# Shifting score rows inside SBUF: each four-tile group by itself, four rows per transfer, in place of two rows over eight tiles

## The reference

```
AC = einsum('bhid,bhjd->bhij', q + u_bias, k)
BD = einsum('bhid,hjd->bhij', q + v_bias, rp)
BD = _rel_shift(BD)                       # row i of BD is shifted by an amount that depends on i
attn = softmax((AC + BD) * scale, axis=-1)
out = einsum('bhij,bhjd->bhid', attn, v)
```

## Time and profile before

| What | Value |
|---|---|
| median of three executions | 3201.2 us (3196.62 to 3203.26) |
| the profiled execution, its own time | 3208.71 us |
| its span, first to last instruction | 3206.9 us |
| mean granted TensorE clock | 0.948 |
| TensorE busy | 91% of the span |
| VectorE busy | 82% |
| ScalarE busy | 78% |
| GpSimd busy (nearly all of it DMA issues of L663) | 72% |
| the shifts' share of the 16 DMA engines | 62.1% of the span |

### The profile page before, as it was taken

How to read it: one execution, slowest core, us unless ns; L and a number is a source line. 1 busy time by engine, 2 the same in 40 slices (tenths; PEclk the granted TensorE clock), 3 DMA queues, 4 the chain that set the end, 5 groups by cost and what they waited for, 6 DMA issues and landing times. The chain is left out here.

```text
span 3206.9 us, 110520 instructions
## 1 busy us (share of the span) xinstructions
PE 2906.8 (91%) x40768; PEld 2051.1 (64%) x40768; DVE 2634.9 (82%) x5042; ACT 2496.0 (78%) x3850; POOL 2310.1 (72%) x4135
## 2 busy tenths in 40 slices
PE   4655479999999999998999999999999999999955
PEld 1444237777777676776777776777767777777645
DVE  2555149899999899997999998999989999999976
ACT  2333368898888898987888898988888889889732
POOL 3333388888888878887878888888878888888800
PEclk8777679999999999999999999999999999999977
DMA  6233678888888878887888888888888888888831
GB/s 201 86 111 111 137 204 224 224 229 229 227 231 222 231 214 228 222 230 194 227 220 227 227 227 220 228 226 224 225 222 223 227 227 226 228 225 222 214 123 53
DMA packets 290222, 657.31 MB, mean 205 GB/s; under 512 B 189473, under 2 KB 256929, under 8 KB 272289
## 3 DMA queue, kind: packets, MB, share of 16 engines
q0 software_dynamic: 190960, 526.89, 62.1%
q1 hardware_dynamic: 98736, 123.38, 13.2%
HBM read 77.19 MB, written 46.14 MB: 38 GB/s over the span
## 5 line engine op out<-in xcount | busy, mean ns | idle before, releaser
L663 POOL DMA_DIRECT2D score<-score x3999 | 2178.4, 548 | 512.4 <-ACT score L902 442.3
L900 ACT COPY score<-pos_bank 128x512 f32<-128x512 f32 x2048 | 1104.2, 597 | 305.1 <-PE pos_bank L776 303.1
L910 ACT ACTIVATE score<-score,low 128x1024 f32<-128x1024 f32 x1024 | 1197.0, 1170 | 36.3 <-DVE low L963 30.2
L972 DVE COPY prob_t<-pt_bank 128x512 f32<-128x512 f32 x1792 | 1162.2, 684 | 7.9 <-PE pt_bank L842 4.0
L842 PE MATMUL pt_bank<-ident_sb,score 128*128 128x128 f32 x8192 | 1085.4, 275 | 10.8 <-issue 6.5
L842 PEld LDWEIGHTS pt_bank<-ident_sb,score 128*128 128x128 f32 x8192 | 953.5, 142 | 218.2 <-DVE prob_t L972 47.2
L963 DVE CUSTOM_DVE_ANT_0 score<-ac_bank,score 128x1024 f32<-128x1024 f32 x512 | 627.1, 1225 | 245.4 <-PE ac_bank L828 126.7
L776 PE MATMUL pos_bank<-pos,qv 96*32 96x512 bf16 (+15 forms) x12160 | 661.2, 317 | 49.9 <-DMA qv<-qv_parts 42.8
L963 DVE CUSTOM_DVE_ANT_0 score<-ac_bank,score,low 128x1024 f32<-128x1024 f32 x512 | 657.2, 1284 | 56.4 <-PE ac_bank L828 47.6
L856 PE MATMUL acc_bank<-prob_t,vs 128*32 128x128 f32 x16384 | 663.5, 279 | 3.5 <-issue 3.4
L828 PE MATMUL ac_bank<-ks,qu 96*128 96x512 bf16 x2048 | 623.9, 386 | 24.7 <-DVE low L963 24.4
(11 more groups left out here) (95 smaller groups left out, 995.6 us busy)
## 6 DMA issues: line engine op xcount, KB each, us to landing
score<-score POOLq DMA_DIRECT2D x3937, 129.5 KB, 5.1
pos<-pos_parts SPq DMA_DIRECT2D x96, 128.0 KB, 8.5
qv<-qv_parts SPq DMA_DIRECT2D x192, 64.0 KB, 7.2
ks<-k_parts SPq DMA_DIRECT2D x192, 64.0 KB, 7.3
qu<-qu_parts SPq DMA_DIRECT2D x192, 64.0 KB, 7.1
v_heads<-v_sb SPq DMA_DIRECT2D x8, 1024.0 KB, 7.3
vs<-v_heads SPq DMA_DIRECT2D x32, 256.0 KB, 8.0
pos_parts<-part SPq DMA_DIRECT2D x16, 384.0 KB, 3.0
```

Of the source, the lines that this page charges most:

```text
L663: pool.dma_start(shifted(odd, s, groups, 0), shifted(odd, s, groups, QUAD - 1 - s))\
L900: act.copy(score[:, at + f, c * BANK:(c + 1) * BANK], ring(m)[:, :]).then_inc(pos_out, 1)
L910: act.activation(cols, cols, ACT.Exp, bias=low[:, slot(k), NH - 1:NH], scale=-1.0)\
L972: dve.tensor_copy(prob_t[:, c, :], PT[c % 2][:, :]).then_inc(copied, 1)
```

## The change

`move` now shifts group j alone, all four partitions with the same s (s, 32 + s, 64 + s, 96 + s) in one transfer: 4 partitions x 1 group, again 4 pieces of 33,152 bytes. Four semaphores, one for each group of the ring, take the place of the four of the even and odd strips. The added last call goes away, so GpSimd issues 128 x 31 = 3968 transfers and not 3999. `add` waits once, for the transfers of its own group. Nothing else is changed.

```
-            moved = [[sem(f"moved{i}_{'even' if odd == 0 else 'odd'}") for i in range(RING // 2)] for odd in range(2)]
+            moved = [sem(f"moved{i}") for i in range(RING)]
...
             def rows_moved(step, n):
-                return (step * (NT // FT // RING) + n // 2 + 1) * (16 * MOVES)
+                return (step * (NT // FT // RING) + n // RING + 1) * (16 * MOVES)
...
             @block.gpsimd
             def _(pool):
-                def shifted(odd, s, groups, first):
-
-                    rows = score[odd * QUAD + s::2 * QUAD, :, :].rearrange("p (g f) w -> p g (f w)", f=FT)
-                    return rows[:, groups, first:first + (FT - 1) * MWIN + L]
-
-                def move(step, j, last=False):
-
-                    if not last:
-                        wait_apart(pool, pos_out, group(step, j) * ITEMS + ITEMS)
-                    odd = 1 if last else 1 - j % 2
-                    n = (j + 1) // 2 if odd else j // 2
+                def move(step, j):
+
+                    wait_apart(pool, pos_out, group(step, j) * ITEMS + ITEMS)
                     at = j % RING
-                    if last or j == 0 and isinstance(step, int) and step == 0:
-                        groups = slice(at, at + 1)
-                    elif at == 0:
-                        groups = slice(0, RING, RING - 1)
-                    else:
-                        groups = slice(at - 1, at + 1)
                     for s in MOVE_ORDER:
                         if s < QUAD - 1:
-                            pool.dma_start(shifted(odd, s, groups, 0), shifted(odd, s, groups, QUAD - 1 - s))\
-                                .then_inc(moved[odd][n % 2], 16)
-                for j in range(RING):
-                    move(0, j)
+                            rows = score[s::QUAD, at * FT:(at + 1) * FT, :].rearrange("p f w -> p (f w)")
+                            width = (FT - 1) * MWIN + L
+                            pool.dma_start(rows[:, 0:width], rows[:, QUAD - 1 - s:QUAD - 1 - s + width])\
+                                .then_inc(moved[at], 16)
                 with pool.Fori(0, STEPS) as step:
-                    for j in range(RING, RING + NT // FT):
+                    for j in range(NT // FT):
                         move(step, j)
-                for j in range(RING, GROUPS - STEPS * (NT // FT)):
+                for j in range(GROUPS - STEPS * (NT // FT)):
                     move(STEPS, j)
-                move(STEPS, GROUPS - STEPS * (NT // FT) - 1, last=True)
...
                     if h == 0 and k % FT == 0:
-                        for odd in range(2):
-                            n = (k // FT + odd) // 2
-                            dve.wait_ge(moved[odd][n % 2], rows_moved(step, n))
+                        dve.wait_ge(moved[k // FT % RING], rows_moved(step, k // FT))
```

## The result

The changed kernel takes 3439.1 us (median of four executions, 3404.5 to 3448.6) where the kernel before takes 3202.2 beside it: a ratio of 1.071, 95% interval 1.068 to 1.075. It is 237 us slower; the forecast was 64. The sign was right and the time lies in the stated range, but the size and the reason for it were wrong.

The account below looks back on a forecast made before the run. TensorE with its partners bounds the kernel before; after the change the DMA engines would, at 15.5 x 1.25 + 1.9 = 21.3 us per group. That swallows the savings and adds 64 to 3201: 3265 us, range 3155 to 3520.

Parts of the forecast that it names:

- Bound of the kernel before: TensorE with its partners at 20.37 us: In the attention, TensorE with its partners sets the pace, 20.37 us per undisturbed group of four tiles; DMA engines nearest behind.
- Start, -15.6: VectorE's first addition needs only call 0 of the shifts, so it moves from 433.04 to about 417.4: -15.6 us.
- Waits in the steady part, -20: VectorE's 47.3 us of waits for shifts all go, as calls come one period earlier; worth -20 us, bounds 0 and -47.
- Instructions, 0: GpSimd issues 31 fewer transfers and VectorE's second wait goes, worth nothing; an issue stays at 547 ns.
- Rival C: GpSimd needs longer to issue for four engines than for two, up to 682 ns: 3317 us; chance 0.04.
- The transfers' engine time, factor 1.25: Shifts' DMA engine time per MB rises by a factor of 1.25, from 60 to about 75 us; ends 1.0 and 2.0.
- quarter of the crowding of the operand loads: Operand loads crowded on 16 neighbouring partitions took a factor of 2.0; a quarter of that extra was taken for the shifts.
- "More than 20.7, the DMA engines are the bound", +64: DMA work of 21.3 us per group exceeds 20.7, so the last group's addition waits for its shifts: +64 us, savings swallowed.
- rival A: The DMA engines don't hinder each other, factor under 1.20, both savings stand: 3166 us; chance 0.36.
- What would show it: Signs: about 75 us per MB, DMA share 0.97, landings over 5.1, VectorE's waits over 100 us, GpSimd's shorter, TensorE less busy.
- B: The shifts' engine time rises by the full factor of 2.0, 32.9 us per group: 4750 us; chance 0.08.

Follow-up runs that it names:

- before_start: Kernel before, but call 0 shifts all four strips of group 0 and call 1 the rest of group 1, then as before; ratio 1.001.
- after_three: Changed kernel with the fourth tile of each group left unshifted, so it leaves work out; ratio 0.992.
- after_small_loads: Changed kernel with operand loads of q, k and positions cut to 64 columns after the first two in each loop pass; ratio 0.999.
- near: Kernel before with rows s and 32 + s (or 64 + s and 96 + s) in one transfer, in place of rows 64 apart; ratio 1.236.
- before_cross: Kernel before with transfers pairing rows s with 96 + s, and 32 + s with 64 + s; ratio 1.001.
- before_pairs: Kernel before with only the order of the transfers changed, to s = 0, 1, 4, 5, ... 28, 29, then 2, 3, 6, 7, ...; ratio 1.184.
- after_tile: Changed kernel with each piece of 33,152 bytes cut into pieces of 8,192 bytes; ratio 1.068.
- before_sems: Kernel before with ten increments of a semaphore nobody waits for behind each turn on TensorE, 160 to a group; slower by 38%.

## Why the prediction was right or wrong

- *Bound of the kernel before: TensorE with its partners at 20.37 us.* Right, and it stays so: the undisturbed groups of the changed kernel take 20.37 as well.
- *Start, -15.6.* Half right: -10.6. The issue was as forecast, but the landings of the first call took 10.5 us (median of the issues between 393 and 412) and not 5.1. The prediction said that one more microsecond could be borne. It was worth nothing in the end: ten groups later the changed kernel is 17.3 us behind (657.62 against 640.28), and before_start shows the gain given back even where the calls behind land as before.
- *Waits in the steady part, -20.* The waits went, all of them, as forecast. They were worth at most 0.8% together with the start and a clock of 1.00 (after_three), and nothing in after_small_loads.
- *Instructions, 0.* Right; 560 ns and not 547, 17.4 us of 20.4. The fewer issues and the fewer waits cost and brought nothing that shows. Rival C is out.
- *The transfers' engine time, factor 1.25.* Right: 1.20, 72.7 us/MB, just over the 72 below which the forecast would have been wrong. The cause, two engines at one place of a side of 64, is shown by near, before_cross and before_pairs. The prediction's quarter of the crowding of the operand loads was a guess that came near, at 1.25; the figure of the Trainium skill's page, 1.22, was nearer.
- *"More than 20.7, the DMA engines are the bound", +64: this is the step that failed.* The work of the engines was forecast at 21.3 us a group, and it is (0.817 + 0.112) x 22.87 = 21.2. Two misses cancel in that: the shifts' factor was 1.20, and the other queues, carried over at 1.9 us, took 0.112 x 22.87 = 2.6, since the hardware queue's engine time rose too, from 56.6 to 74.7 us per MB (0.101 x 2300 x 16 / 49.73). With 1.20 and 1.9 the sum would have given 20.5 us and no loss, rival A; with 21.2 it gives 394 + 128 x 21.2 + 6 = 3114 and +52. So even with the measured work the step misses most of the 237, and that 3439 lies in the range is luck. For the engines did not become the bound: their share is 0.93, VectorE never waits for a shift, GpSimd's wait for the copies grew from 381 to 523 us where it was to shrink, and a group takes 22.87 us, 1.6 more than the engines need. The cost reached the time by another way, which the prediction did not have among its rivals: longer landings, TensorE standing still for its code for 1.30 us more a group, and its clock at half for 8.5% of the time, which makes 0.83 us more busy time. A queue that is nearly full was treated as harmless until it is full. After_three at 0.91 without loss and after_tile at 0.98 with no more loss than the changed kernel show that the share of the engines, on which the sum was built, is not the measure.
- *What would show it.* Right: engine time per MB, landings over 5.1, TensorE's busy share. Wrong: DMA share of 0.97, VectorE's wait over 100 us, GpSimd's shorter wait. Those three wrong signs say that the mechanism is another, though the sign of the time was right.

Rival A, no hindrance, fails on the 1.20; its own threshold was a factor under 1.20, so the measured one lies right on it, and its 3166 us would still have been wrong. B would have needed 2.0.

## What to carry to other kernels

Put the transfers that run at the same time on different places: rows on both sides of partition 64, and neighbours in the queue four rows apart as in the kernel before; with the same bytes and the same number of transfers, the pairing of rows was worth 24% here and their order 18%. Where the DMA engines are as busy as here (0.84 in the kernel before), read the longest landing and the engines' idle time that ends in "issue" before and after a change, and not only the share and the waits for data. A gain at the start is one only if the engine that issues it isn't itself busy without a break.

## What the runs showed of the hardware

- TensorE's code comes through a queue of the same DMA engines as the data, one packet of 16 KB for each 256 instructions (125 for a pass of 32,052), one per 8 us here. Where the longest landing of a shift is 16.4 us, TensorE stalls for up to 6 us at a time, 142 us of 2300: at 55 of the 263 packets it waits over 0.9 us, and at 3 of 289 in the kernel before. The page "Runtime: NRT & Kernel Launch" of the Trainium skill, section "Instruction fetch mechanics", says that an engine's sequencer fetches blocks of 16 KiB, 256 instructions, on its own DMA queue while it executes, at a cost that is mostly hidden. Size and queue agree with the 256 counted here and the 250 of before_sems; hidden holds for the kernel before (13 us) and not for the changed one.
- A stall of a few microseconds can cost more than itself: behind the one of 3.41 us the granted clock is 0.50, and in the group with three stalls the same 313 matmuls were busy for 23.96 us and not 20.37.
- Rows 32 apart on the same side of partition 64 in one transfer cost 1.44 times the engine time (near). Rows 64 or 96 apart, and rows 32 apart across partition 64, cost nothing (60.5 and 60.7 us/MB in the kernel before and before_cross).
- Open: in what way long queues of shifts hold back a packet of code, when the packet itself takes only 1.22 us in the changed kernel and 1.08 before (means) and the length of the pieces doesn't matter. No run separates the queue's own wait from that for the memory it writes.
